# Row maxima and exponentials of two heads in one instruction, and a new order of every engine's calls, in a two-layer attention and FFN kernel

## The reference

```python
x = x + _L0_xattn_ref(ctx, ctx, _layernorm(x), ssm_kernel, D, 8)
x = x + _L0_ffn_ref(_layernorm(x), gate_w, gate_b, val_w, val_b, out_w, out_b)
x = x + _L1_xattn_ref(_layernorm(x), ctx, mask, mask, Wq, bq, Wk, bk, Wv, bv)
x = x + _L1_ffn_ref(_layernorm(x), Wc, temperature, genes, Wd, Wu, norm_w, scale)

# _L1_xattn_ref, the step that the change touches
dot = jnp.einsum('bhdt,bhds->bhts', q, k) / math.sqrt(HEAD_DIM)
dot = mask * dot - (1.0 - mask) * NEG
amap = jax.nn.softmax(dot, axis=-1) * mask
out = jnp.einsum('bhts,bhds->bhdt', amap, v)
# _L1_ffn_ref
logits = jnp.einsum('btd,gd->btg', xn, Wc) / jnp.clip(temperature, 0.1)
top_vals, top_idx = jax.lax.top_k(logits, N_ACTIVE)
```

## Time and profile before

| what | us |
|---|---|
| median of 3 runs | 664.58 (662.44 to 668.01) |
| the profiled execution, its own time | 668.12 |
| its span, first to last instruction | 666.3 |
| first `first_sum` (DVE, L1326) of the loop begins at | 159.7 |
| busy: PE, PEld | 512.2, 246.2 |
| busy: DVE, ACT, POOL | 487.4, 336.2, 379.1 |

### The profile page before, as it was taken

How to read it: one execution, slowest core, us unless ns; L and a number is a source line. 1 busy time by engine, 2 the same in 40 slices (tenths; PEclk the granted TensorE clock), 3 DMA queues, 4 the chain that set the end, 5 groups by cost and what they waited for, 6 DMA issues and landing times.

```text
span 666.3 us, 11825 instructions
## 1 busy us (share of the span) xinstructions
PE 512.2 (77%) x3439; PEld 246.2 (37%) x3439; DVE 487.4 (73%) x984; ACT 336.2 (50%) x686; POOL 379.1 (57%) x644
## 2 busy tenths in 40 slices
PE   0457999991558688888988888888888897789644
PEld 0343333330222343543443443443443443343222
DVE  3572888885336677699999999999998987782342
ACT  1531000000322266577787787787787785576512
POOL 5325656642565465667678678678678546322332
PEclk9958999996666779789999999999999997796955
DMA  8910000001034443463463463463462462411100
GB/s 283 353 27 6 20 23 24 24 19 51 14 78 90 83 102 86 94 136 86 86 143 89 94 134 95 95 144 83 89 151 74 84 145 68 80 37 34 30 16 16
DMA packets 94355, 56.41 MB, mean 85 GB/s; under 512 B 14979, under 2 KB 94020, under 8 KB 94294
## 3 DMA queue, kind: packets, MB, share of 16 engines
q1 hardware_dynamic: 92198, 53.56, 33.8%
q10 hardware_dynamic: 2096, 2.12, 0.9%
HBM read 37.74 MB, written 19.52 MB: 86 GB/s over the span
## 4 chain that ended last, share of the span: by engine, by line
issue 22%; DVE 17%; PE 10%; POOL 10%; DVEq 8%; POOLq 8%; DMA 2%; SPq 1%; ACT 1%
DVE neg_max L1404 8%; PE bank L484 3%; POOLq L862 2%; DVEq L1362 2%; PE bank L444 2%; DVEq L1442 2%; DVEq L1313 2%; POOLq L41 1%; POOL w_raw L911 1%; POOL qT L863 1%; PE bank L379 1%; DVE st L1314 1%; POOL dx L984 1%; POOLq L961 1%; POOL qT L962 1%
## 5 line engine op out<-in xcount | busy, mean ns | idle before, releaser
L1404 DVE TENSOR_REDUCE neg_max<-bank 128x2 f32<-128x512 f32 x256 | 167.1, 681 | 23.4 <-PE bank L444 22.6
L1130 ACT ACTIVATE cT<-bank 128x512 f32<-128x512 f32 x256 | 146.7, 597 | 30.3 <-PE bank L455 29.1
L444 PE MATMUL bank<-KS,w_raw 54*128 54x256 bf16 x512 | 94.6, 289 | 32.0 <-DVE neg_max L1404 24.8
L455 PE MATMUL bank<-w_raw,KS 57*128 57x256 bf16 x512 | 94.8, 289 | 2.3 <-ACT cT L1130 2.1
L315 PE MATMUL bank<-kv,toep 128*128 128x512 f32 x192 | 88.0, 608 | 8.2 <-issue 5.1
L854 POOL TENSOR_TENSOR kv<-cT 128x2048 f32 x16 | 57.5, 3599 | 40.6 <-POOLq L851 40.6
L484 PE MATMUL bank<-cT,v_aug 128*32 128x256 f32 x1024 | 73.7, 408 | 2.4 <-ACT kv L1138 2.4
L444 PEld LDWEIGHTS bank<-KS,w_raw 54*128 54x128 bf16 x512 | 32.1, 96 | 102.6 <-DVE neg_max L1404 63.8
L1072 ACT ACTIVATE qT<-bank 128x256 bf16<-128x256 f32 x16 | 6.2, 385 | 120.2 <-PE bank L375 120.2
L315 PEld LDWEIGHTS bank<-kv,toep 128*128 128x128 f32 x192 | 35.7, 193 | 59.8 <-issue 59.8
L1292 DVE TENSOR_TENSOR w_raw<-bank,qT 128x512 f32<-128x512 f32 x64 | 39.7, 683 | 23.5 <-DVEq L1287 23.5
(11 more groups left out here) (167 smaller groups left out, 1029.1 us busy)
## 6 DMA issues: line engine op xcount, KB each, us to landing
w_raw<-scr_q SPq DMA_DIRECT2D x32, 192.0 KB
KS<-scr_k SPq DMA_DIRECT2D x32, 192.0 KB
scr_o<-kv SPq DMA_DIRECT2D x64, 36.0 KB
yT<-in_x SPq DMA_DIRECT2D x2, 1024.0 KB, 7.1
scr_toeps<-scr_toep ACTq DMA_DIRECT2D x1, 2048.0 KB, 16.0
kv<-in_ctx SPq DMA_DIRECT2D x2, 1024.0 KB, 11.2
toep<-scr_toeps SPq DMA_DIRECT2D x16, 128.0 KB, 2.0
x_b<-in_x SPq DMA_DIRECT2D x16, 128.0 KB, 2.6
```

Source lines behind the costliest of these rows:

```text
L444: return pe.matmul(M[h % 2][:, th * L:(th + 1) * L], QS[b % 3][rows, h // 2, th * P:(th + 1) * P], KS[b % 3][rows, h // 2, :], start=True, ...
L455: return pe.matmul(SC[n % 2][:, sh * L:(sh + 1) * L], KS[b % 3][rows, n // 2, sh * P:(sh + 1) * P], QS[b % 3][rows, n // 2, :], start=True ...
L1130: act.activation(probs[n % 8], SC[n % 2][:], ACT.Exp).then_inc(s(f"scores{n % 2}_free"), 1)
L1404: dve.tensor_reduce(neg_max[:, :, h:h + 1], M[h % 2][:].rearrange("p (t s) -> p t s", s=L), AX.X, ALU.max, negate=True).then_inc(s(f"max{h ...
```

## The change

Banks 0 to 3 become two tensors of two banks each, `pairs[0]` (M) and `pairs[1]` (SC). A group g is two heads. TensorE's `maxima(b, g)` waits until the whole pair is free, makes four matmuls into it, one head in each bank, and signals once; VectorE's `maxima(b, g)` reduces 1024 values to two maxima for each head in one instruction. `scores(b, g)` and `exps(b, g)` do the same with SC, and `probs` holds four pairs in place of eight heads. The pairs have no second buffer: the next group's matmuls wait for the reduction, or the exponentials, of the last. The maxima and the scores run abreast with the other head of their own pair, not with each other. The loop lists of all five engines are in a new order with other distances, and no function of the other stages is changed but for the semaphores' names.

```diff
-        banks = [ctx.enter_context(nc.psum_tensor(f"bank{i}", [P, 512], F32)) for i in range(8)]
+        pairs = [ctx.enter_context(nc.psum_tensor(f"pair{i}", [P, 1024], F32)) for i in range(2)]
+        banks = [pair[:, 512 * i:512 * (i + 1)] for pair in pairs for i in range(2)]
+        banks += [ctx.enter_context(nc.psum_tensor(f"bank{i}", [P, 512], F32)) for i in range(4, 8)]
...
-        M, SC, O, X5, X6, X7 = banks[0:2], banks[2:4], banks[4], banks[5], banks[6], banks[7]
+        M, SC, O, X5, X6, X7 = pairs[0], pairs[1], banks[4], banks[5], banks[6], banks[7]
...
+            def maxima(b, g):
...
+                if b or g:
+                    pe.wait_ge(s("max_free"), GRP * b + g)
+                for th in range(KL):
+                    for j in range(2):
+                        rows, at = tops[j], 2 * L * j + th * L
+                        mm = pe.matmul(M[:, at:at + L], QS[b % 3][rows, g, th * P:(th + 1) * P], KS[b % 3][rows, g, :],
+                                       start=True, stop=True)
+                mm.then_inc(s("max_ready"), 1)
+
+            def scores(b, g):
...
+                if b or g:
+                    pe.wait_ge(s("scores_free"), GRP * b + g)
+                for sh in range(KL):
+                    for j in range(2):
+                        rows, at = stacks[j], 2 * L * j + sh * L
+                        mm = pe.matmul(SC[:, at:at + L], KS[b % 3][rows, g, sh * P:(sh + 1) * P], QS[b % 3][rows, g, :],
+                                       start=True, stop=True)
+                mm.then_inc(s("scores_ready"), 1)
...
+            def exps(b, g):
...
+                done = 4 * b + g // 2 - 1
+                act.wait_ge(s("scores_ready"), GRP * b + g + 1)
+                if g % 2 == 0 and done >= 1:
+                    act.wait_ge(s("o_ready"), done)
+                act.activation(probs[g % 4].rearrange("p j l -> p (j l)"), SC[:], ACT.Exp).then_inc(s("scores_free"), 1)
...
+            def maxima(b, g):
...
+                dve.wait_ge(s("max_ready"), GRP * b + g + 1)
+                dve.tensor_reduce(neg_max[:, :, 2 * g:2 * g + 2].rearrange("p t j -> p j t"),
+                                  M[:].rearrange("p (j t s) -> p j t s", t=KL, s=L), AX.X, ALU.max, negate=True
+                                  ).then_inc(s("max_free"), 1)
```

More of the change, by code:

```diff
@@ L478, in values @@
                     pe.wait_ge(s("x7_free"), turn7["v", b])
-                for k in range(2):
-                    pe.wait_ge(s(f"scores{k}_free"), H // 2 * b + 2 * q + 2)
+                pe.wait_ge(s("scores_free"), GRP * b + 2 * q + 2)
                 take_o("values", b, q)
@@ L557, in _ @@
                 transpose_xr(m - 3)
[L558 to L559 removed]
+                gate(m + 5, 1)
+                maxima(m, 1)
                 logits_product(m - 3)
[L561 to L562 removed]
+                maxima(m, 2)
+                scores(m - 1, 0)
+                value(m + 5, 1)
                 transpose_weights(m - 4)
+                scores(m - 1, 1)
+                maxima(m, 3)
+                project_qk(m + 2)
@@ L574, in _ @@
                 down_up(m - 4)
-                transpose_maxima(m)
+                ffn_product(m + 4)
+                maxima(m, 6)
+                scores(m - 1, 6)
+                values(m - 1, 2)
+                transpose_hidden(m + 5)
+                scores(m - 1, 7)
+                maxima(m, 7)
+                transpose_y(m + 8)
+                gate(m + 6, 0)
+                values(m - 1, 3)
+                project_v(m + 1)
         @block.sync
@@ new lines, in _ @@
+            for m in range(-7, B + 3):
+                exps(m - 1, 6)
+                collect(m - 1, 2)
+                copy_hidden_T(m + 5, 0)
+                exps(m - 1, 7)
+                copy_hidden_T(m + 5, 1)
+                tanh_gate(m + 6, 0)
+                collect(m - 1, 3)
+                exp_logits(m - 3)
+                value_operand(m + 1)
+                copy_max_rows(m)
+                copy_value(m + 6, 0)
+                copy_xrT(m - 2)
+                tanh_gate(m + 6, 1)
+                exp_left(m - 3)
+                copy_logits(m - 2)
+                exps(m, 0)
+                copy_value(m + 6, 1)
+                exps(m, 1)
+                copy_wT(m - 3)
+                exps(m, 2)
+                collect(m, 0)
+                exps(m, 3)
+                copy_xqT(m + 7)
+                copy_exprT(m - 3)
+                exps(m, 4)
+                collect(m, 1)
+                exps(m, 5)
+                quantise_hidden(m + 6)
+                tanh_down(m - 3)
@@ new lines, in _ @@
+            for m in range(-13, B):
+                bias_and_mask_qk(m + 7)
+                top_next(m + 2, 1)
+                maxima(m + 5, 4)
+                top_strike(m + 2, 1)
+                hidden_scales(m + 10)
+                maxima(m + 5, 5)
+                top_next(m + 2, 2)
+                top_strike(m + 2, 2)
+                second_sum(m + 9)
+                top_bias(m + 2)
+                maxima(m + 5, 6)
+                statistics_x3(m + 3)
+                down_times_up(m + 1)
+                scale_x(m + 12)
+                maxima(m + 5, 7)
+                first_sum(m + 13)
+                statistics_x2(m + 9)
+                top_next(m + 2, 3)
+                open_gate(m + 11, 0)
+                maxima(m + 6, 0)
+                top_strike(m + 2, 3)
+                statistics_x1(m + 13)
+                maxima(m + 6, 1)
+                open_gate(m + 11, 1)
+                inverse_weight_sum(m + 2)
+                maxima(m + 6, 2)
+                top_first(m + 3)
+                top_strike(m + 3, 0)
+                inverse_denominators(m + 4)
+                maxima(m + 6, 3)
```

231 lines of the change are left out of this document (50 added, 181 removed).

## The result

The changed kernel takes 657.88 us (median of 4 runs, 654.13 to 658.46) against 664.55 us for the kernel before beside it (4 runs, 662.44 to 668.01): a ratio of 0.988, with a 95% interval of 0.983 to 0.993. It is about 1.2% faster. I had forecast 675 us, 17 too many, and given "faster" 0.22. The profiled execution took 654.13 us with a span of 652.3 us; it is the fastest of its four, 3.8 us under their median, where the profiled execution of before lay 3.5 us above its own (668.12 against 664.58).

What follows compares the result with a forecast made beforehand. The prediction took VectorE to bound the middle and something else the two ends. It summed 242 us to the first maximum, 367.7 of maxima and 68 of tail to a 677.7 us span, said as 675 us; range 650 to 692.

Steps and rivals of the forecast that it cites:

- rival 1: Freed ends outweigh the longer ramp: TensorE's clock stays high there, five turns of 12.2 us; median 645 us; chance 0.22.
- samples 0 to 2: First three samples' maxima: 22.5 us each, 67.5 in all, where each took about 24 before; bounds 19 and 25.
- samples 11 to 15: Last five samples' maxima, with no FFN beside them: 21.5 us each, 107.5 in all; bounds 19.5 and 23.3.
- tail: Stretch after the last maximum: 68 us against 71.8, about 4 less before den32, then 36 unchanged; bounds 62 and 74.
- rival 2: Gains and losses cancel: samples 0 to 2 at 21 us, 11 to 15 at 20.5; total 666 us; chance 0.20.
- The longer ramp: Turns before the first maximum: 12.6 + 3 x 14.3 + 16.5 = 72 us after 170, first maximum at 242, 38 later.
- the way of the maxima: From a sample's last maximum to its next scores, through split, transpose, copy, issues and landing: 5.7 us, within turns of 21.5.
- Samples 8 to 10: Three samples' maxima while the FFN's calls drop out one by one: 24.3, 22.9 and 22 us.
- The full period: Middle turns, one sample entering and one leaving: 24.9 us becomes 24.4 by wide reduces, 24.7 with 0.3 of waits.
- The 0.06 us a pair: VectorE's wide reduce against two narrow ones, 1.13 us for 1.19; 0.5 us a period, 8 us over 128 pairs.
- The cover of the refill: Refilling a single pair costs about 0.55 us, hidden by VectorE's other calls between maxima, 0.7 us at the thinnest.
- Rival 3: A missed fill of a single pair idles VectorE 1.5 us in each of eleven FFN periods; 691 us; chance 0.16.

Runs made afterwards that it cites:

- experiment 6: From the changed kernel, every call of the FFN, its statistics and its loads one turn later, six turns from first_sum to the maxima, not seven; 645.07 us, ratio 0.972.
- Experiment 9: The kernel before, narrow instructions and order as they were, with the FFN's calls one turn earlier; 674.99 us, ratio 1.015.
- experiment 1: The changed kernel in its own order, with each wide reduce and each wide exponential issued as two of 512; 663.78 us, ratio 0.999.
- experiment 2: The changed kernel with only the reduces narrow (two of 512), the exponentials wide; 664.16 us, ratio 0.997.
- experiment 3: The changed kernel with only the exponentials narrow, the reduces wide; 655.21 us, ratio 0.985.
- experiment 5: The changed kernel with the second open_gate moved ahead of the second maxima of a turn; 660.56 us, ratio 0.995.
- experiment 4: The kernel before in its old order, with the pairs of banks and the wide instructions, scores two groups behind the maxima; 682.76 us, ratio 1.031.

## Why the prediction was wrong

The direction was wrong. By its numbers it is rival 1 that came nearest: it had the first maximum at 231, samples 0 to 2 in 58.5 us, samples 11 to 15 in 100 and a tail of 65, 646.5 in all; the trace has 233.7, 61.5, 100.0 and 63.0, 652.3 in all. The median is 658, on the border to rival 2. Its mechanism came in part only: TensorE's clock did not stay at its upper level in the ramp (0.75 on the mean from 159.7 to 233.7 us), and not every turn cost the hidden chain alone. Its five turns of 12.2 fit the 62.2 us of the ramp because shorter turns and a longer one made up for each other.

**The step that failed** is the one in "The longer ramp" that reads "GpSimd ties a longer one: `statistics_x2` now stands behind `first_sum` ... 14.3 us", with 3 x 14.3 and the 16.5 of the last turn in the sum. In the changed kernel the five turns took 12.4, 11.4, 11.7, 12.6 and 14.1 us, together 62.2 against 72. The instructions and their times were right. Two things were not.

First, the sample. In the changed lists `normalise_x2(m + 6)` stands on GpSimd ahead of `gate_times_value(m + 9, 0)`, three samples apart, and `statistics_x2(m + 9)` on VectorE ahead of `open_gate(m + 11, 0)`, two apart. The normalisation is of a sample whose statistics are a turn old, so it waits for nothing and can fill a gap of GpSimd's. I had followed the order of the names within a turn and not the offsets. In experiment 6, where the two are of one turn, the rows show the wait that I had priced; what it is worth there stays open.

Second, which turns hold the work. I gave a whole turn's work of GpSimd's to all of them, but the ramp fills up sample by sample: in the second turn GpSimd has neither a normalisation of x2 nor a `split_qk` and is busy 6.75 us, in the third it has no `split_qk`, and only the fifth has it all (12.27 us). In the second and third turn `first_sum` waits 2.10 us for TensorE's transposed y: there the hidden layer's chain holds the turn, at 11.4 and 11.7 us and not 12.6 as worked out from the first turn. In the fourth and fifth it is GpSimd that comes last, by its sum and not by the chain that I drew. It goes from one first product to the next, 14.1 us later, with no wait but short gaps at its drains, and `first_sum` waits for its `add_output_bias`, 2.93 us and 1.63 us. The 14.2 us that the prediction gives as GpSimd's sum in such a turn with `split_qk` was therefore right, for one turn. The V projection's 2 us did not come on top of it.

```profile
207.43 1.26 POOL L901 TENSOR_TENSOR w_raw<-w_raw 128x512 f32<-128x512 f32 x1 [1.15 <-ACT w_raw L1076]
...
221.51 1.26 POOL L901 TENSOR_TENSOR w_raw<-w_raw 128x512 f32<-128x512 f32 x1
```

```profile
204.13 0.42 DVE L1307 TENSOR_TENSOR qT<-bank,x_b 128x256 f32<-128x256 f32 x1 [2.10 <-PE bank L365]
...
217.56 0.42 DVE L1307 TENSOR_TENSOR qT<-bank,x_b 128x256 f32<-128x256 f32 x1 [2.93 <-POOL qT L869]
...
231.65 0.42 DVE L1307 TENSOR_TENSOR qT<-bank,x_b 128x256 f32<-128x256 f32 x1 [1.63 <-POOL qT L869]
```

**Terms that were mis-sized.**
- Samples 0 to 2: 22.5 forecast, 18.5, 20.4 and 22.6 measured. I had built them at a mean clock of 0.79 plus the way of the maxima; with the chain cut the clock was 0.82 for the first and 1.00 for the second, and the bound of 19 was the better guess for the first. Experiment 9 cuts the same chain in the old order and shows turns of 21.2 to 21.7 for 23.8 to 24.1. Over all three samples the mean clock was 0.94; what the cut chain gave and what the clock gave was not told apart.
- Samples 11 to 15: 21.5 forecast, and 21.5, 20.4, 20.3, 20.4 and 17.4 measured. The sum over these five was 7.5 us too long, and 4.1 of that is a slip of counting: the stretch ends at the last maximum, so sample 15 is no whole turn. In the others the way of the maxima was priced with one piece after the other. That the rest of this turn is a chain through `down_times_xr`, x3's normalisation and `split_maxima` was only read from the trace of after, not tested.
- Samples 8 to 10: 1.8 us too short, and not looked into.
- Tail: 68 forecast, 63.0 measured. From the last maximum to den32 it is 27.8 us where it had been 35.9 (8 less, forecast 4); from there on 35.2 against 36, as forecast. The mean clock of the tail was 0.80 where it had been 0.67.

**What held.** The full period: 24.7 forecast, 24.3 to 25.0 measured, and no wait of VectorE's maxima for a fill from 340 to 440 us. The 0.06 us a pair: experiments 1 and 2 find the width worth 1%, about 6 us over 128 pairs, against 8 forecast. The 16 us that I had worked out by the Trainium skill (VectorE: DVE Perf Modes, the trn2 errata) did not appear, neither in the rows nor in the totals. That exponentials gain nothing (experiment 3). The cover of the refill, the thinnest gap included: experiment 5 opens it and finds a wait of 0.42 us, against 0.55 forecast. Rival 3 did not come, yet experiment 4 shows a like loss in the order of before, at 20 us. The rule of the Trainium skill that spoke against the change (PSUM — Partial Sum Buffer, summary of rules: while matmuls run, read only from a bank other than theirs) can be weighed by two kernels: with both banks shut during each wide read, the old order with wide calls pays 3% (experiment 4), while in the new one VectorE waits for no fill from 393 to 418 us.

Failures of different kinds, then. One was a chain given to turns that don't hold it, by a misread offset and by counting full turns where the pipeline was still filling: 7.2 of the 10 us between the 72 and the 62.2 lie in the three turns of 14.3, and 2.4 in the last. The other was that I took the low clock of the old ramp and the old end into stretches where it turned out higher (0.94 over samples 0 to 2, 0.97 over samples 11 to 15); that the cut chain raised it is a guess. The lower bounds that the prediction itself names (233, 19, 19.5, a tail of 62) would have summed to 233 + 57 + 123.5 + 69.2 + 97.5 + 62 = 642.2 us; the measured 652.3 lies 10 above that and 25 below the forecast.

## What to carry to other kernels

In a software pipeline, follow the sample index and not only the order of the calls: a step waits within the turn for another only if what it needs was made in that turn. For the turns that fill the pipeline, write down which stages already have a sample, and sum only those. Here a pair of banks read by one wide instruction saved time only on the engine that was the bound, and only in the order in which each refill had other calls of that engine in front of it, so lay the order first and widen second. And once the order is made, try each stage one turn closer: here the distance chosen was one too long, and one less gave more than the whole change had (0.972 against 0.988).

## What the runs showed of the hardware

- A reduce of 1024 values from two neighbouring banks takes 1215 ns and lets the next call start 1.11 to 1.14 us after it; two reduces of 512 take 1.19. An exponential of 1024 takes 1024 ns where one of 512 took 597.
- From the end of a reduce to the start of the waiting matmul is about 0.06 us, and four matmuls of 256 columns into a pair take 0.39 us. Nearly uncovered that is a wait of 0.42 us (experiment 5).
- The mean granted clock of the profiled executions rose from 0.880 to 0.923, but it is not by itself a measure of the gain: experiment 1 had 0.910 and took as long as the kernel before. It was at 0.97 in a ramp turn in which TensorE was busy 7.3 of 12.6 us, and at 0.62 in one in which it was busy 11.1 of 15.1 (experiment 6), with 39 instructions in both, so that the lower level itself makes the busy time longer. What raised it was not found out.
